# A hybrid attention and mixture-of-experts network: the tie penalty of the first attention written in another algebra

## What is computed

```
S = relu(att[:, 0]); S[..., 0] = 0; S = S * (1 - eye)
FF = cumsum(shift(S), axis=1)
att = att - FF[:, None]
rank = argsort(argsort(where(causal, FF, inf)))     # per row
keep = rank < min(409 - 1, i + 1)  or on the diagonal
att = where(keep, att, -inf)
y = softmax(att) @ v
```

## Time and profile before

| | us |
|---|---|
| median of 3 runs | 2950.25 |
| lowest and highest run | 2947.14, 2955.3 |
| the profiled execution's own time | 2931.04 |
| its span | 2929.3 |
| PE busy (89% of the span) | 2600.9 |
| DVE busy (63%) | 1844.5 |
| ACT busy (61%) | 1783.4 |
| POOL busy (12%) | 345.6 |
| mean granted clock of TensorE, share of full | 0.944 |

### The profile page before, as it was taken

How to read it: one execution, slowest core, us unless ns; L and a number is a source line. 1 busy time by engine, 2 the same in 40 slices (tenths; PEclk the granted TensorE clock), 3 DMA queues, 4 the chain that set the end, 5 groups by cost and what they waited for, 6 DMA issues and landing times. The chain is left out here.

```text
span 2929.3 us, 75687 instructions
## 1 busy us (share of the span) xinstructions
PE 2600.9 (89%) x31004; PEld 1627.1 (56%) x31004; DVE 1844.5 (63%) x5181; ACT 1783.4 (61%) x3488; POOL 345.6 (12%) x718
## 2 busy tenths in 40 slices
PE   8999878888889799999998989999999999896596
PEld 3677756666666452212213546676676767665355
DVE  6999887887886662100002757877777787663862
ACT  3676655565666338999996246666666667531331
POOL 2100142222221010000000100000000000026026
PEclk7998989999999899999998999999999999898598
DMA  3410010111100202100000010000000000303003
GB/s 117 69 27 2 2 17 17 18 17 17 17 11 3 53 1 91 58 19 1 1 1 17 1 40 7 2 7 7 3 7 7 7 2 2 98 14 49 29 15 58
DMA packets 85120, 68.23 MB, mean 23 GB/s; under 512 B 40776, under 2 KB 73688, under 8 KB 84392
## 3 DMA queue, kind: packets, MB, share of 16 engines
q1 hardware_dynamic: 76328, 57.09, 8.3%
q0 software_dynamic: 8448, 6.30, 1.7%
HBM read 47.21 MB, written 19.96 MB: 23 GB/s over the span
## 5 line engine op out<-in xcount | busy, mean ns | idle before, releaser
L1769 ACT ACTIVATE arena<-ps 128x1024 f32<-128x1024 f32 x512 | 474.1, 1282 | 25.9 <-PE ps L1719 24.0
L1220 DVE CUSTOM_DVE_ANT_0 arena<-ps,arena 128x1024 f32<-128x1024 f32 (+7 forms) x384 | 350.0, 931 | 105.0 <-PE ps L1096 88.5
L2147 DVE CUSTOM_DVE_ANT_0 arena<-ps,arena 128x512 f32<-128x512 f32 (+3 forms) x640 | 371.2, 643 | 26.7 <-PE ps L2011 25.8
L1172 ACT ACTIVATE arena<-ps 128x1024 f32<-128x1024 f32 (+3 forms) x320 | 275.0, 896 | 129.1 <-PE ps L1129 125.7
L2104 ACT ACTIVATE arena<-arena 128x1152 f32<-128x1152 f32 (+15 forms) x256 | 306.4, 1199 | 63.2 <-DVE arena L2147 63.2
L2011 PE MATMUL ps<-arena 64*128 64x512 f32 (+3 forms) x1280 | 270.3, 547 | 3.5 <-ACT arena L2080 1.1
L1730 PE MATMUL ps<-arena 128*32 128x512 f32 x2048 | 273.0, 604 | 0.0
L2042 PE MATMUL ps<-arena 128*64 128x128 f32 x4352 | 262.3, 275 | 0.0
L2042 PEld LDWEIGHTS ps<-arena 128*64 128x64 f32 x4352 | 235.3, 137 | 33.4 <-issue 28.7
L923 PE MATMUL ps<-arena 128*128 128x256 bf16 (+1 forms) x2176 | 238.1, 273 | 13.7 <-DVE arena L895 9.2
L2066 ACT COPY arena<-ps 128x512 f32<-128x512 f32 (+3 forms) x410 | 189.6, 517 | 75.8 <-PE ps L2028 73.6
(11 more groups left out here) (301 smaller groups left out, 4026.4 us busy)
## 6 DMA issues: line engine op xcount, KB each, us to landing
arena<-scr_q SPq DMA_DIRECT2D x256, 32.0 KB
scr_s<-scr_f SPq DMA_DIRECT2D x1, 4096.0 KB, 16.5
arena<-scr_k SPq DMA_DIRECT2D x32, 128.0 KB
arena<-by_head_k SPq DMA_DIRECT2D x16, 192.0 KB
arena<-scr_s SPq DMA_DIRECT2D x16, 192.0 KB, 2.6
arena<-by_head_q SPq DMA_DIRECT2D x28, 96.0 KB
by_head_k<-arena SPq DMA_DIRECT2D x5, 512.0 KB, 4.5
scr_x<-arena SPq DMA_DIRECT2D x2, 1024.0 KB, 5.2
```

The source lines that it names most:

```text
L1172: e.activation(turned_block(u, kc), src, ACT.Exp, scale=-1.0).then_inc(exped, 1)
L1220: e.tensor_tensor_reduce(scored_block(u, g)[:, lo:hi], PS[:, 1024 * (k % 2):1024 * (k % 2) + hi - lo], NF[t][:, lo:hi], -1.0, mxs[:, col - ...
L1769: e.activation(PTR[k % RS], PS[:, at(n):at(n) + 1024], ACT.Sigmoid, scale=float(1 / np.sqrt(8.0))).then_inc(weighed, 1)
L2147: e.tensor_tensor_reduce(slot(u, t, g)[:, lo:hi], PS[:, base(step) + 512 * g:base(step) + 512 * g + hi - lo], bias, -1.0, mxs[:, col - 1:c ...
```

## The change

j = 4 becomes a `tensor_scalar` that reads only the running count: it gives -TINY (minus 2 to the power -126) where the count exceeds `need`, and minus zero elsewhere, in bf16, whether the column is a tie or not. j = 5 then compares the difference to the threshold with that number: FF - threshold > -TINY is true above the threshold and, at a tie (difference zero), where the mark is set. j = 6 reads the result from the other buffer.

```diff
+TINY = float(2.0 ** -126)
...
                 if j == 4:
-                    e.scalar_tensor_tensor(CS[:, 0:W], CS[:, 0:W], nd, E[:, 0:W], ALU.is_gt, ALU.mult).then_inc(penalty, 1)
+                    e.tensor_scalar(E[:, 0:W], CS[:, 0:W], nd, -TINY, ALU.is_gt, ALU.mult).then_inc(penalty, 1)
                 if j == 5:
-                    e.scalar_tensor_tensor(E[:, 0:W], nf, th, CS[:, 0:W], ALU.is_gt, ALU.max).then_inc(penalty, 1)
+                    e.scalar_tensor_tensor(CS[:, 0:W], nf, th, E[:, 0:W], ALU.subtract, ALU.is_gt).then_inc(penalty, 1)
                 if j == 6:
-                    e.scalar_tensor_tensor(nf, E[:, 0:W], NEG, nf, ALU.mult, ALU.subtract).then_inc(penalty, 1)
+                    e.scalar_tensor_tensor(nf, CS[:, 0:W], NEG, nf, ALU.mult, ALU.subtract).then_inc(penalty, 1)
```

## The result

| | before | after |
|---|---|---|
| median, us | 2951.65 (2945.99 to 2962.35, 14 runs) | 2943.1 (2935.8 to 2953.69, 14 runs) |
| profiled execution, us | 2931.04 | 2936.74 |
| its span, us; mean granted clock | 2929.3 | 2935.0; 0.947 |

The ratio of the medians is 0.9972 with a 95% interval of 0.9961 to 0.9983: 8.3 us less, between 5.0 and 11.5. That is just within the 0.3% that the forecast calls "no change it can tell"; the forecast was 7.0 us less. A second set of runs (experiment 4) gave 0.9971.

What follows compares the result with a forecast made beforehand. In the attend part PE and DVE were nearly evenly busy, so neither alone was the bound. Gains of 0.8 + 3.7 + 2.5 = 7.0 us off the 2950.25 us median gave 2943.2 us, range 2935 to 2951.

Steps and rivals of the forecast that it cites:

- The new instruction's price: The 13 new j = 4 instructions on DVE take 7.1 us instead of 20.1, judged from line 895.
- j = 5 and j = 6: These two-tensor DVE instructions keep their 20.1 and 19.4 us, within 0.7 us each.
- Tile 7: At tile 7 the shorter j = 4 lets PE, waiting for POOL's splits, start 0.8 us earlier.
- Tile 15: At tile 15 POOL's splits slip through before line 1038 starts, so PE starts 3.7 us earlier.
- this term, at 2.3 us: From 389 to 396 us, behind tile 15's stall, the clock may stay up: worth 2.3 us.
- all of it arrives: Rival: all 13.0 us of saved DVE work arrives, plus tile 15 and clock extras: 9 to 17 us, chance 0.35.
- Tiles 14, 13, 3, 8: DVE runs without a gap behind j = 4 until PE has waited for it; those waits are gained: 2.5 us.
- The seven covered tiles: Tiles 12, 4, 11, 5, 10, 6, 9: 6.4 us saved, but covered by PE's own work, so 0 gained.
- the first rival: All 13.0 us of saved DVE work arrives, with extras: 9 to 17 us, 2941 to 2933, chance 0.35.
- The sum: Gains in the attend part, 0.8 + 3.7 + 2.5 = 7.0 us, taken off the median.
- The signs that I named: New profile: j = 4 at 7.1 us, no 4 us POOL wait, line 1220 waits about 20, attend part 7 us earlier.
- the stretch behind keeps its length: The stretch behind the attend part should not change its length by more than a few us.

Runs made afterwards that it cites:

- experiment 4: The changed kernel run again unaltered, for a second trace: 2946.39 us, ratio 0.9971 to the kernel before.
- experiment 2: The kernel before with the new j = 4 to 6 at the twelve tiles other than tile 15: 2953.78 us, ratio 0.9998.
- experiment 3: The kernel before with the new form only at tiles 12, 4, 11, 5, 10, 6 and 9: 2957.24 us, ratio 1.0005.
- experiment 11: The kernel before, old j = 4 kept, with the planner told the measured cost of each extra instruction: 2920.25 us, ratio 0.9975.
- experiment 1: The kernel before with the new j = 4 to 6 at tile 15 alone: 2949.78 us, ratio 0.9983.
- experiment 5: The changed kernel with tile 15's new j = 4 issued as four instructions of 512 columns: 2919.94 us, ratio 0.9968 to the kernel before.
- experiment 6: The changed kernel with j = 4 on one column at all 13 tiles (wrong at ties): 2920.07 us, ratio 0.9966 to the kernel before.
- experiment 9: The kernel before with tile 15's old j = 4 issued as four instructions of 512 columns: 2923.68 us, ratio 0.9985.
- experiment 7: The changed kernel with the extra instructions hung one score piece later by the planner: 2913.74 us, ratio 0.9954 to the kernel before.
- experiment 8: The changed kernel with the planner told the measured cost of each extra instruction: 2911.11 us, ratio 0.9936 to the kernel before.

## Why the prediction was right, point by point

**The new instruction's price: right.** 7.2 us for the 13, with 352 and 751 ns at the ends, against a forecast of 7.1, 350 and 750. Taking it from line 895, which has the same operand types and other operations, was good to 0.1 us. **j = 5 and j = 6: right**, 20.1 and 19.4 us to the digit, with the new mixtures of types.

**Tile 7: right**, 0.80 for 0.8.

**Tile 15: right in its mechanism, too small in its size.** The splits slipped through with PE 3.66 us earlier, for 3.7 forecast. But the place gave 5.34. The further 1.7 us come behind it, over the stretch in which PE had half clock before (0.51) and has full clock now (1.00). I had this term, at 2.3 us, but put it into the rival "all of it arrives" instead of the sum. It does not belong there: it follows from the removed stall and not from the covered tiles. That this step is the clock is read from ten traces. Four have a wait of 3.9 to 4.1 us here (before, experiments 2, 3 and 11), and in all four 6.8 us of half clock begin inside it. Six have a wait of 1.5 us or less (after, experiments 1, 4, 5, 6 and 9), and none has low clock here; experiment 9 among them has no part of the change. No edit moves the clock alone; none was tried.

**Tiles 14, 13, 3, 8: forecast 2.5, measured 1.55.** 0.73 for 1.05, 0.67 for 0.72 (ACT takes over after, as I warned), 0.15 for 0.35, and 0 for 0.38. The step that failed is "I take these waits as gained", and with it the test in front of it, that DVE runs without a gap behind j = 4. A gap of zero before doesn't say how long the next scores had been ready. At tile 8 they came only just in time: now DVE waits 0.81 us for them, all but 0.1 of the 0.90 saved, and so the 0.38 further on stands as before. At tile 14 it waits 0.60 of the 1.49 saved, and only what is left reaches PE's first wait; the second (0.45) stays. These two tiles are in part or wholly of the covered kind, which the trace of before didn't show as idle time.

**The seven covered tiles: right.** Their lead falls back, but for tile 11's, where the clock made the difference; DVE's idle time at tile 4 grew by the saved 0.50, and experiment 3 excludes their 6.4 us. This is what puts the first rival down, with experiment 2 (11.4 us of DVE work for 0.6 us) and the pair of 5 and 6 (4.8 us of work for 0.1 us).

**The sum: 7.0 forecast, 7.7 in steps that repeat, 8.3 and 8.6 in the medians.** Two errors stand against each other, +1.7 at tile 15 and -1.0 at the four tiles, so that it is in part luck that the sum came so near. Medians with intervals of 3 us each way don't tell 7.0 from 8.3. At 0.28% the result lies just beside the line between "within 0.3%" and "faster".

**The signs that I named.** j = 4 at 7.1 us, j = 5 and j = 6 unchanged, no 4 us wait at tile 15: all came. PE's wait for line 1220 was to fall from 23.2 to about 20; it fell to 22.8. That sign was badly chosen: at tiles 14 and 8 PE's waits for line 1221 stayed at their length because PE and DVE moved together. The attend part was to end 7 us earlier; it was 9.4 and 9.9. The sign "the stretch behind keeps its length" failed in the single trace (870 us to the end is 2065.0 us against 2059.3, with the attend part over some 12 us earlier) for the reason given above: the stages behind the attend part, none of which the change touches, are 18 to 25 us shorter in before's trace than in the five of after and experiments 1 to 4. Taking 7.0 off the median and not off the profiled execution was the right choice.

**Open.** Whether tile 15's other long wait, 3.38 us behind the scan j = 3, would also go if that scan were cut in pieces; it wasn't tried. How much of the 0.6 to 1 us between the repeating steps and the medians is clock; through which step experiment 7 shortens the waits for ACT; and why experiment 8's costs give what they do, since no single wait of PE that they shorten is as large as the gain.

## What to carry to other kernels

The worth of this shorter instruction was not its saved time but what it holds: more than half of this gain was one chain of four tiny POOL instructions that now fit between two long DVE ones, and cutting the old instruction in four pieces at that one place gave half the gain while adding work. So look first for small instructions whose duration equals that of a long neighbour, and ask whether the order, or a cut, can let them by. A wait that stands behind a busy engine is an upper bound of the gain, and an engine without a gap may still have got its input at the last moment. And where a static planner sets the order, tell it the measured cost of each step: here that and hanging the steps one piece later together gave more (0.9898 against 0.9971) than the faster instruction did.

## What the runs showed of the hardware that was not expected

- A POOL instruction of 2 columns that starts behind the start of one of DVE's j = 2 to 6 lasts until that one instruction's end, and is let go between two back-to-back DVE instructions: 2.25 us beside one of 2.35, 0.65 and three times 0.58 to 0.59 beside four that take 2.74 together. In the traces of before and after this holds for every one that starts 0.05 us or more behind and has 0.25 us or more of the DVE instruction beside it; those that start at most 0.03 us behind, or ahead of the DVE instruction, take their 0.20 us.
- Two kinds of DVE instruction don't hold it. Beside j = 0 (744 to 2343 ns, one tensor in and a count out) all 21 take 0.19 or 0.20 us, and so do those beside the score add of line 1221, which reads PSUM and SBUF (0.20 us at 386.66, beside the add of 1.22 us from 386.44, in the changed kernel).
- In the four traces with a stall of 3.9 to 4.1 us on PE at tile 15, 6.8 us at the lower granted clock begin inside it; in the six where the stall is 1.5 us or less the clock stays up. The stall's price was 3.7 us for itself and about 1.7 us behind it.
- The granted clock falls at other places, or for another length, in each execution of the same program, and moved single steps of the lead by 1 to 3 us. Two profiled executions of the changed kernel differ by 8.6 us, and the stages that the change doesn't touch by 18 to 25 us between the trace of before and those of its set. Totals of single traces can't carry a verdict of this size, and a step that repeats in two traces needs one of before with the same clock at its place.
